# Differential attention and a ternary feed-forward part on one core: when the weights are rounded, and how the last pair of tiles is worked off

## The reference

```python
x = x + attn(layernorm(x))          # q, k with rope; 32 score maps, causal softmax
#   diff = probs[:, :, 0] - lambda_full * probs[:, :, 1]
#   attn = diff @ v, rms-normalised per head, * subln_weight * (1 - LAMBDA_INIT), @ Wo.T
h = layernorm(x)
scale = mean(abs(w)); wq = sign(w) * (abs(w) >= 0.7 * scale)     # for w1 and for w2
x = x + gelu(h @ w1q.T + b1) @ w2q.T + b2
```

## Time and profile before

| | us |
|---|---|
| median of 3 runs | 4198.97 |
| lowest and highest run | 4195.23, 4203.26 |
| the profiled execution, its own time | 4199.09 |
| its span, first to last instruction | 4197.2 |
| PE busy in the span | 3491.2 (83%) |
| DVE busy | 3189.3 (76%) |
| ACT busy | 2885.2 (69%) |
| POOL busy | 1776.2 (42%) |
| mean granted TensorE clock | 0.943 |

### The profile page before, as it was taken

One profiled execution on the slowest core, in us unless ns is written; L12 is line 12 of the kernel. 1 busy time (PEld: TensorE's weight loads), 2 busy tenths in 40 slices (PEclk: granted clock), 3 DMA queues, 4 the chain that ended last, 5 costly groups with the idle time before them and its releaser, 6 DMA issues.

```text
span 4197.2 us, 84069 instructions
## 1 busy us (share of the span) xinstructions
PE 3491.2 (83%) x23454; PEld 2099.4 (50%) x23454; DVE 3189.3 (76%) x5170; ACT 2885.2 (69%) x6784; POOL 1776.2 (42%) x2333
## 2 busy tenths in 40 slices
PE   2688888888888888888888888888888888888886
PEld 1355554555444555455545555555545555555553
DVE  6777877778678886788767887778867778677882
ACT  1577766777667775677766777667766777667772
POOL 1244443454334543345432544334443444334543
PEclk6899999999999999999999999999999999999999
DMA  3101011000011001000011010111001010110000
GB/s 133 38 19 34 20 34 34 29 20 26 29 34 34 18 28 38 29 25 29 21 34 34 20 34 16 36 31 34 20 30 34 22 31 20 35 34 29 20 28 14
DMA packets 146840, 128.57 MB, mean 31 GB/s; under 512 B 66608, under 2 KB 117680, under 8 KB 145840
## 3 DMA queue, kind: packets, MB, share of 16 engines
q1 hardware_dynamic: 146352, 122.79, 9.1%
HBM read 67.61 MB, written 55.12 MB: 29 GB/s over the span
## 4 chain that ended last, share of the span: by engine, by line
PE 42%; DVE 22%; issue 19%; ACT 12%; POOL 2%; ACTq 1%; DVEq 1%; DMA 1%; SPq 0%; POOLq 0%
PE M L864 9%; PE F L936 7%; DVE NM L707 7%; PE SP_ L879 6%; PE M L914 5%; PE F L953 5%; PE DP L891 4%; DVE NM L715 4%; DVE E L734 3%; ACT E L579 3%; ACT DT L591 2%; PE M L858 2%; ACT L579 2%; ACT L596 1%; PE DX L891 1%
## 5 line engine op out<-in xcount | busy, mean ns | idle before, releaser
L579 ACT ACTIVATE E<-SP_,NM 128x256 f32<-128x256 f32 (+7 forms) x2048 | 1523.5, 744 | 922.6 <-DVE NM L715 527.2
L707 DVE TENSOR_REDUCE NM<-SP_ 128x1 f32<-128x896 f32 (+3 forms) x1024 | 1031.7, 1018 | 291.9 <-PE SP_ L880 286.5
L879 PE MATMUL SP_<-KST,QST 96*128 96x512 f16 (+3 forms) x3072 | 828.2, 341 | 372.1 <-ACT E L579 316.0
L734 DVE SCALAR_TENSOR_TENSOR E<-E,CC 128x512 f32<-128x512 f32 (+7 forms) x1024 | 941.4, 919 | 49.3 <-POOL CC L494 30.0
L891 PE MATMUL DP<-ident,E 128*128 128x128 f32 x3328 | 569.6, 286 | 85.7 <-DVE E L734 76.2
L879 PEld LDWEIGHTS SP_<-KST,QST 96*128 96x128 f16 x3072 | 274.4, 101 | 712.4 <-ACT E L579 487.1
L591 ACT ACTIVATE DT<-DP 128x512 f32<-128x512 f32 (+3 forms) x1024 | 525.7, 513 | 123.2 <-PE DP L891 117.0
L491 POOL TENSOR_TENSOR RP<-SUM,minus 128x1 f32<-128x1 f32 x512 | 292.5, 571 | 722.5 <-ACT E L579 708.2
L715 DVE TENSOR_REDUCE NM<-SP_ 128x2 f32<-128x1024 f32 (+3 forms) x512 | 419.2, 819 | 198.9 <-PE SP_ L880 188.9
L864 PE MATMUL M<-WQKV,WT 128*128 128x512 f32 x1040 | 546.0, 618 | 17.9 <-DVE TOK L775 11.0
L936 PE MATMUL F<-X2H,W1Q 128*128 128x256 f16 x2048 | 499.6, 282 | 31.3 <-DVE SQ L803 16.6
(11 more groups left out here) (96 smaller groups left out, 4847.3 us busy)
## 6 DMA issues: line engine op xcount, KB each, us to landing
scratch<-SPL SPq DMA_DIRECT2D x65, 576.0 KB, 2.8
QST<-scratch SPq DMA_DIRECT2D x390, 64.0 KB, 2.4
X<-in_x SPq DMA_DIRECT2D x66, 256.0 KB, 2.8
out<-SQ SPq DMA_DIRECT2D x64, 256.0 KB, 2.0
KST<-scratch SPq DMA_DIRECT2D x390, 32.0 KB, 1.9
DT<-in_w2T SPq DMA_DIRECT2D x1, 4096.0 KB, 25.9
KST<-in_w1T SPq DMA_DIRECT2D x2, 1024.0 KB, 10.6
WQKV<-in_wqT SPq DMA_DIRECT2D x1, 1024.0 KB, 6.6
```

The costliest lines, as they stand in the source:

```text
L579: act.activation(dst, score_out(i, 2 * n + k, w), ACT.Exp, bias=NM[:, (2 * u + k) % 8:(2 * u + k) % 8 + 1], scale=1.0, accum_out=SUM[:, i ...
L707: nc.vector.tensor_reduce(NM[:, m:m + 1], score_out(i, 2 * n + k, P * (i + 1)), AX.X, ALU.max, negate=True).then_inc(max_ready, 1)
L734: nc.vector.scalar_tensor_tensor(out=E1[:, u % 4, 0:w], in0=E2[:, u % 2, 0:w], scalar=CC[:, u % 4:u % 4 + 1], in1=E1[:, u % 4, 0:w], op0=A ...
L879: pe.matmul(SP_[:, k[a // 512], 0:n], q, KST[0:ROWS, a // P:(a + n) // P, kk, :], start=True, stop=not last)
```

## The change

It has two parts. Part one is about the start and the first three blocks:
- DVE clears `QST`, as its first instruction. DVE normalises tile 0 before it scales the query weights, and each load has a semaphore of its own.
- The raw weights move: w1 to `DT` (first half), `KST` (second half, tiles 4 to 7) and `X1`; w2 to `DT` (second half), `HH` and `HL`. `stack(0)` no longer waits for w1. w2, WO and the biases are loaded behind it.
- ACT takes the sums of absolute values (`abs_chunk`, Abs with an accumulator, 2048 columns each): w1's in the start, w2's at hs 2, 6, 10 and 14 of block 1.
- In the start DVE rounds only two quarters of w1. The other two follow as four halves (`late_cut`) at hs 4, 10, 18 and 26 of block 0, and w2 as eight halves in block 2. WO's scaling, the sum and the thresholds of w2 go into block 1. PE waits for all roundings before the first `first_product` (block 3, hs 1), SP for six of them before it stacks into tile 4 of `KST`.

Part two is about the last pair, which leaves the blocks: `every_block` puts out two last blocks instead of three. After them the pair goes through in eight pieces. A first product of two feature blocks goes into one of the four banks of `SP_`, ACT does bias and GELU in one instruction straight from the bank, DVE (even pieces) or POOL (odd) splits, and the second products of both tiles accumulate side by side in `F` and `DP`, two pieces behind the first products. b2 is added to the residual ahead of time, and each tile has an output buffer of its own.

The core of the diff (new tiles `ones` of 128 columns and `wsum` of 8, f32, and the new semaphores are left out):

```diff
+ABS_AT = (2, 6, 10, 14)
+CUT_AT = ((0, 4), (0, 10), (0, 18), (0, 26)) + tuple((2, hs) for hs in (1, 5, 8, 11, 15, 18, 22, 26))
+WO_AT, ABS_TOTAL, ABS_PRODUCT, THR_AT = 8, 18, 20, 22
...
-        self.w1 = t % 2 == 1 and runs(3, (1,))
-        self.w2 = t % 2 == 0 and runs(4, (0, 2))
+        self.w1 = t % 2 == 1 and runs(3, ())
+        self.w2 = t % 2 == 0 and runs(4, (0,))
...
-    for t in range(3):
+    for t in range(2):
         run(QBlock(B, t, "last"))
...
+                if T.raw and t == TILES // 2 - 1:
+                    sp.wait_ge(cut_done, 6)
...
-            sp.wait_ge(w1_cut, 1)
             sp.wait_ge(q_zeros, 1)
             stack(0, 0, 0, None)
+            sp.dma_start(WO[:, :, :], woT.rearrange("k p n -> p k n")).then_inc(wo_in, 16)
...
+            for k in range(4):
+                sp.dma_start(w2f[k].rearrange("p (k n) -> p k n", k=FT // 4),
...
-            pool.memset(QST[:, :, :, :], 0.0).then_inc(q_zeros, 1)
...
+            for k in range(1, FT // 2, 2):
+                h, fs = end_rows(k)
+                pool.wait_ge(end_gelu, k + 1)
+                hold(pool, f2_ready, 2 * LAST)
+                pool.tensor_scalar(HH[:, fs, :], HP[:, h, :], 1.0, 0.0, ALU.mult, ALU.add).then_inc(end_high[1], 1)
+                pool.wait_ge(end_high[1], k // 2 + 1)
+                pool.tensor_tensor(HL[:, fs, :], HP[:, h, :], HH[:, fs, :], ALU.subtract).then_inc(end_split[1], 1)
...
+            def abs_chunk(j, k):
+                act.wait_ge(raw_in[j][k], 16)
...
+                act.activation(HP[:, :, :].rearrange("p a b -> p (a b)"), raw[j][k], ACT.Abs,
+                               accum_out=wsum[:, j, k:k + 1]).then_inc(abs_part, 1)
...
             xt_copy(0, 0)
+            for k in range(4):
+                abs_chunk(0, k)
             high(0, 0)
...
+            for k in range(FT // 2):
+                h, fs = end_rows(k)
+                act.wait_ge(end_f1, k + 1)
...
+                for j in range(2):
+                    ins = act.activation(HP[:, h.start + j, :], SP_[:, k % 4, 2 * P * j:2 * P * j + 2 * P], ACT.Gelu,
+                                         bias=b1c[:, fs.start + j:fs.start + j + 1], scale=1.0 / XS)
...
+            def late_cut(n):
+                j, k, c = (n + 4) // 8, (n + 4) // 2 % 4, slice(FF // 2 * (n % 2), FF // 2 * (n % 2) + FF // 2)
...
+                link(nc.vector.tensor_scalar(low[:, n // 2 % 2, c], raw[j][k][:, c], thr[:, j, 1:2], None, ALU.is_le))
+                nc.vector.scalar_tensor_tensor(out=cut[j][:, FF * k + c.start:FF * k + c.stop], in0=raw[j][k][:, c],
...
+            nc.vector.memset(QST[:, :, :, :], 0.0).then_inc(q_zeros, 1)
...
+            abs_total(0)
+            thresholds(0)
...
+            for k in range(2):
+                link(nc.vector.tensor_scalar(low[:, k, :], raw[0][k], thr[:, 0, 1:2], None, ALU.is_le))
+                cut_chunk(0, k, low[:, k, :])
...
+            def end_second(k):
+                pe.wait_ge(end_split[k % 2], k // 2 + 1)
+                for j in range(2):
+                    for f in (2 * k, 2 * k + 1):
+                        for hp in (HH, HL):
+                            ins = pe.matmul((F, DP)[j][:, :], hp[:, f, P * j:P * (j + 1)], W2Q[:, f, :],
...
+            for k in range(FT // 2):
+                end_first(k)
+                if k == 2:
+                    pe.wait_ge(o_sum, 2 * LAST)
+                    pe.wait_ge(dt_ready, B * N_T)
+                if k >= 2:
+                    end_second(k - 2)
+            end_second(FT // 2 - 2)
+            end_second(FT // 2 - 1)
```

More of the change, by code:

```diff
@@ L139, in __init__ @@
         self.finish = runs(1, (0,))
-        self.w1 = t % 2 == 1 and runs(3, (1,))
-        self.w2 = t % 2 == 0 and runs(4, (0, 2))
+        self.w1 = t % 2 == 1 and runs(3, ())
+        self.w2 = t % 2 == 0 and runs(4, (0,))
+        self.end = kind == "last" and t == 1
         self.nb = b * TILES + t + 1
@@ L146, in __init__ @@
         self.next = (t + 1) % TILES
+        self.raw = kind == "first"
     def before(self, n):
@@ L216, in diff_attention_ffn @@
         thr = sb("thr", [P, 2, 2], F32)
+        ones = sb("ones", [P, P], F32)
+        wsum = sb("wsum", [P, 2, 4], F32)
         KST = sb("KST", [P, TILES, NK // 2, P], F16)
@@ L260, in diff_attention_ffn @@
         scratch = nc.dram_tensor("scratch", [2, P, 3, D + DKV], F16, kind="Internal").ap()
-        qkv_in = sem("qkv_in")
-        w_in = sem("w_in")
-        w1_in = sem("w1_in")
-        w2_in = sem("w2_in")
+        wq_in = sem("wq_in")
+        kv_in = sem("kv_in")
+        rope_in = sem("rope_in")
+        lam_in = sem("lam_in")
+        wo_in = sem("wo_in")
+        raw_in = [[sem(f"w{j + 1}_in_{k}") for k in range(4)] for j in range(2)]
+        abs_part = sem("abs_part")
+        thr_ready = sem("thr_ready")
+        cut_done = sem("cut_done")
+        wo_ready = sem("wo_ready")
+        neglam_ready = sem("neglam_ready")
         pool_const = sem("pool_const")
@@ L273, in diff_attention_ffn @@
         wq_scaled = sem("wq_scaled")
-        w1_cut = sem("w1_cut")
-        ready = sem("ready")
         x_in = [sem("x_in_even"), sem("x_in_odd")]
@@ L444, in _ @@
             pool.memset(maskb[:, :], 0.0).then_inc(pool_const, 1)
-            pool.memset(onesf, 1.0).then_inc(pool_const, 1)
-            pool.memset(QST[:, :, :, :], 0.0).then_inc(q_zeros, 1)
+            pool.memset(ones[:, :], 1.0).then_inc(pool_const, 1)
             pool.memset(minus1[:, :], -1.0)
@@ L850, in _ @@
+            dve.wait_ge(neglam_ready, 1)
             every_block(dve, dve_work)
+            for j in range(2):
+                x1 = X1[:, (TILES - 2 + j) % 4, :]
+                nc.vector.tensor_tensor(x1, x1, b2b[:, :], ALU.add).then_inc(end_res, 1)
+            for k in range(0, FT // 2, 2):
+                h, fs = end_rows(k)
+                dve.wait_ge(end_gelu, k + 1)
+                dve.wait_ge(f2_ready, 2 * LAST)
+                nc.vector.tensor_copy(HH[:, fs, :], HP[:, h, :]).then_inc(end_high[0], 1)
+                dve.wait_ge(end_high[0], k // 2 + 1)
+                nc.vector.tensor_tensor(HL[:, fs, :], HP[:, h, :], HH[:, fs, :], ALU.subtract).then_inc(end_split[0], 1)
@@ L853, in _ @@
+            dve.wait_ge(end_res, 2)
+            dve.wait_ge(o_out, 16 * (N_TILES - 2))
+            for j in range(2):
+                dve.wait_ge(end_f2, j + 1)
+                nc.vector.tensor_tensor((OUT, TOK)[j][:, :], (F, DP)[j][:, :], X1[:, (TILES - 2 + j) % 4, :],
+                                        ALU.add).then_inc(end_out, 1)
         @block.tensor
@@ L956, in second_product, with abs_product @@
                     ins.then_inc(f2_ready, 1)
+            def abs_product(j):
+                pe.wait_ge(abs_sum, j + 1)
+                pe.matmul(F[:, j:j + 1], ones[:, :], wtot[:, j:j + 1], start=True, stop=True).then_inc(abs_all, 1)
             def pe_work(T):
@@ L1038, in _, with end_first @@
             transposes(T1[:, D:D + DKV], 2, m_kt)
-            for j in range(2):
-                after(pe, abs_sum, j + 1)
-                pe.matmul((F, M)[j][:, 0:1], onesf, wtot[:, j:j + 1], start=True, stop=True).then_inc(abs_all, 1)
-            pe.wait_ge(ready, 3)
+            abs_product(0)
             every_block(pe, pe_work)
+            def end_first(k):
+                if k >= 4:
+                    pe.wait_ge(end_gelu, k - 3)
+                for f in (2 * k, 2 * k + 1):
+                    for c in range(KD):
+                        for xp in (X2H, X2L):
+                            ins = pe.matmul(SP_[:, k % 4, 2 * P * (f % 2):2 * P * (f % 2) + 2 * P], W1Q[:, c, P * f:P * (f + 1)],
+                                            xp[:, c, :], start=(c == 0 and xp is X2H), stop=(c == KD - 1 and xp is X2L))
+                ins.then_inc(end_f1, 1)
+            def end_second(k):
+                pe.wait_ge(end_split[k % 2], k // 2 + 1)
+                for j in range(2):
+                    for f in (2 * k, 2 * k + 1):
+                        for hp in (HH, HL):
+                            ins = pe.matmul((F, DP)[j][:, :], hp[:, f, P * j:P * (j + 1)], W2Q[:, f, :],
+                                            start=(f == 0 and hp is HH), stop=(f == FT - 1 and hp is HL))
+                    if k == FT // 2 - 1:
+                        ins.then_inc(end_f2, 1)
+            pe.wait_ge(x2_ready, N_TILES)
+            pe.wait_ge(exp_done, B * N_E)
+            for k in range(FT // 2):
[7 more added lines that the diff above has]
+            end_second(FT // 2 - 1)
 def rope_tables():
```

132 lines of the change are left out of this document (83 added, 49 removed).

## The result

| | before | after |
|---|---|---|
| median, us | 4197.1 | 4138.59 |
| lowest and highest, us | 4194.09, 4203.26 | 4135.7, 4140.81 |
| the profiled execution, its span, us | 4197.2 | 4133.9 |
| mean granted TensorE clock | 0.943 | 0.949 |

The ratio is 0.9857, with a 95% interval from 0.9842 to 0.9873. I had predicted 4155.5 us and a range of 4146 to 4166. The profiled execution of after (4135.7 us) is the fastest of its four, 2.9 us under the median, and that of before (4199.09) lies 2.0 above its median, so the steps read from the two profiles add up to 63.3 us, 4.8 more than the medians differ by.

What follows compares the result with a forecast made beforehand. At the start DVE alone was taken to bound (busy 50.42 of 53.2 us); at the end, work passing between engines. Start -44.0, blocks +23.1, end -22.5 sum to -43.4 on 4198.97: 4155.5 us, range 4146 to 4166.

Steps and rivals of the forecast that it cites:

- The loop of batches 1 to 7 is not edited, and I cost it at nothing: Hardware loop after the first blocks: its code is unchanged, so its time was forecast to change by 0 us.
- rival E: Loop: new tiles shift addresses by 544 bytes and slow accesses; at 1 us a tile 4219 us; chance 0.02.
- Start: Program start to first scores: scores at 42.4 instead of 86.39 us, a gain of 44.0, range 43 to 48.
- The clearing: Start: DVE's clearing of QST takes 9.1 us, range 5.1 to 9.1, so tile 0's statistics begin 2.7 us earlier.
- Hidden, with 2 us to spare: Start: ACT's Abs of w1 end by 26 us, before ACT is wanted at about 28, so they cost nothing.
- Blocks 0 to 2: Cost of rounding work moved into the first three blocks: 4.3 + 5.7 + 13.1 = 23.1 us, between 13 and 33.
- rival A: Blocks 0 to 2 absorb nothing, every moved instruction is paid for: cost 33.6 us, time 4166; chance 0.14.
- Last pair: End of the program: PE runs through eight pieces without waiting, ending at 4174.7; gain 22.5 us, ends 19 and 24.
- the cold one: Last pair: the first group of matmuls runs at the lower clock, adding 1.4 us.
- C: Start and block 1: Abs is not in Exp's table, so each brings two 1.28 us loads; 4165 us; chance 0.03.
- D: Last pair: PE stays at the lower clock, 27.8 us more, the end gains nothing; 4183 us; chance 0.02.
- B: Start and blocks: cheap clearing gives 4 us, more slack in the blocks 6; time 4146; chance 0.12.

Runs made afterwards that it cites:

- s3: The kernel before plus two unused tiles (512 and 32 bytes per partition) that shift later tiles as in the change; no instruction differs: 4195.87 us, ratio 0.9999.
- s7: The kernel after with ScalarE's copies of the high parts placed between the four Abs of w1 instead of behind them: 4137.64 us, ratio 0.9850.
- s8: s7 with the comparisons of the twelve half roundings on POOL and 24 idle increments on VectorE: 4139.99 us, ratio 0.9854.
- s11: s7 plus 48 idle semaphore increments on VectorE while it waits for lambda: 4131.36 us, ratio 0.9835.
- s2: The kernel before with only the new last pair (part two); nothing ahead of the loop changed: 4175.69 us, ratio 0.9944.
- s15: The kernel after plus 48 idle semaphore increments on VectorE while it waits for lambda, nothing else: 4135.60 us, ratio 0.9853.
- s16: The kernel after, unchanged, measured and profiled a second time: 4137.21 us, ratio 0.9852.
- s1: The kernel after with the old last pair, so only part one (start and rounding) of the change: 4159.33 us, ratio 0.9902.
- s12: The kernel after with all first products of the last pair sent into one bank instead of four: 4145.02 us, ratio 0.9863.

## Why the prediction missed

**The step that failed** is the term "The loop of batches 1 to 7 is not edited, and I cost it at nothing". It was about -12 us, not 0: 8.5 to 12.8 by the medians of the four kernels with increments alone, 13.3 by the mean of the two sets of loops, and 18.5 between the two profiles. With -12 in the sum, 4155.5 would have been 4143.5, within 5 us of the median. My own list had "if batches 1 to 7 differ in length" as a sign of being wrong. I looked for a mechanism only on the slow side, as a shift of data addresses (rival E), and s3 shows that one to be worth nothing. What moved was the place of VectorE's code: 16 instructions more ahead of the loop put its fixed stops at other instructions.

**Start, right in sum (44.0 against 44.7), wrong in its terms.** The clearing took 3.47 us, not 9.1; my range had 5.1 as its lower end and named the quarter below it without using it. The Trainium skill, "VectorE: DVE Perf Modes", section "Zero memsets can be issued as uint32 (trn2)", gave both halves, one cycle per element and half the elements. The row agrees with the second, 4096 words. For the first it has 0.85 ns per word, less than VectorE's plain pace of 1.12 ns per element (2286 ns for 2048). Most of the 5 us gained were lost again to lambda's loads and to ScalarE's order: w1 landed up to 4 us later than I took, and "Hidden, with 2 us to spare" was not so. From the first stack to the scores it took 9.8 us (31.90 to 41.72) against 10.7. VectorE was free at 39.4, I had 39.6.

**Blocks 0 to 2, 20.6 against 23.1.** Block 0 paid 3.4 us for three halves of 2.03, where I had 4.3. Block 2 is right by two errors. Seven halves of 2.03 us lie in its stretch, 14.2 us, not eight of 2.1; and VectorE absorbed next to none of them: it rests 59.97 - 52.29 = 7.7 us after and 46.70 - 38.59 = 8.1 before. VectorE's work is paid for in full there, as rival A said, at a lower price and one half less. Block 1 cost 3.9 where I had 5.7. ScalarE is busy 7.3 us longer in it (29.15 for 21.88) with the four Abs, and VectorE 4.4 us (33.42 for 29.00): the last half of w1 falls behind stack 1, so into this stretch, and WO's scaling took 2.10 us and not 1.3. Which of the two engines the 3.9 us are paid for is not shown.

**Last pair, 21.0 against 22.5.** No wait between the pieces, pace and tail as forecast. The term that was too small is the cold one, 3.1 us instead of 1.4: the higher clock came only 6.0 us after PE had begun. That is a matter of the execution more than of the step: with the same chain the first three groups took 8.3 us in after, s7, s8 and s11, but 6.9 to 7.1 in s2, s15 and s16, a surcharge of 1.7 to 1.8. In s16, the same kernel, the last pair took 33.5 us, 22.4 less than before, against my 22.5. What I did not allow for is that the surcharge varies.

**The rivals.** C is out (Abs 1.91 us, no table load), D is out (clock 1.00 from 4105.9 on); its price was too low, since 27.8 us more would have made the end 5 us longer, not equal. E is out by s3. B had the cheap clearing right and its effect wrong. None ended below 4146, and so the range didn't either: it held what I knew to be uncertain, and nothing for code that is merely moved.

## What to carry to other kernels

When an edit ahead of a long hardware loop changes an engine's number of instructions, measure the loop by itself in both profiles; here the place of VectorE's code alone was worth 0.3%, over a quarter of the gain forecast, and 16 idle instructions in a wait tested it. Take more than one profile for that: two of one kernel differed by 5.9 us in the loop. A gain on one engine at the start is worth only what the next late thing leaves: list the landings of all loads in their new order before taking it. Where an engine is as full as VectorE was in block 2 (38.6 of 46.7 us), count moved work at its full price.

## What the runs showed of the hardware

- VectorE: the length of a loop of 1336 instructions depends on the place of its code. It was 3483.2 us in the mean at one place (moved by 0, 128 and 256), and 3470.0 in the mean of three others (16, 32, 64). The stops that tell the places apart, 0.1 to 0.4 us long, stand at multiples of 128 instructions plus a constant, in the same rows every round. 19 instructions more on ScalarE had no effect, 4199.63 against 4199.43.
- VectorE clears 8192 f16 per partition in 3.47 us, as 4096 words; POOL took 6.92.
- POOL compares 128x1024 f32 against a threshold per partition in 3.7 us, VectorE in 0.74.
- Four executions of one kernel lay up to 17 us apart: s1 took 4152.06 at a mean granted clock of 0.949, and 4169.12 at 0.944.
- TensorE, at 1.2 GHz at the head of the last pair, worked without a rest and rose to 2.4 GHz 6.0 us later in one execution of the kernel after, 3.2 us later in another. In s12, with two rests of 1 us, it was still at 1.2 GHz after 12.5 us.
